# Query parts written before the key spreads, late units of a recurrence over four PSUM banks, and fills placed behind each product at a change of stage

## The chip, the cores and the metric

One core of one Trainium2 chip runs the whole program. The metric is the device time of one execution in microseconds (us); the profile is one execution taken by the hardware profiler. Engines: PE (TensorE), DVE (VectorE), ACT (ScalarE), POOL (GpSimd), SP (SyncE, which issues nearly all the DMAs); the five run their own instruction streams and meet at semaphores.

## What is computed

Four layers in a row on x of shape (4, 256, 256), each with the same context; `attend` is softmax attention with a maximum taken per row.

```python
# layer 0: 16 heads of 16, keys and values from the normalised context
Q, K, V = x @ Wq.T, ln(ctx) @ Wk.T, ln(ctx) @ Wv.T
x = x + tanh(gate) * attend(Q, K, V) @ Wo.T
# layer 1: a linear recurrence over the 256 positions, 32 heads of 8x8 state
def step(s, inp):
    a = k_l[..., :, None] * v_l[..., None, :]
    out = einsum('bhs,bhst->bht', r_l, faaaa * a + s)
    return a + w_l[..., None] * s, out
y = groupnorm(scan(step)) * gn_w + gn_b
x = x + (y * g) @ Wo.T
xc = ln(x); xk2, xr2 = mix(xc)          # with the row before
x = x + sigmoid(xr2 @ fWr.T) * (square(relu(xk2 @ fWk.T)) @ fWv.T)
# layer 2: 32 query heads of 8 on 8 key heads, additive mask, then a layer norm
# layer 3: two attentions, 16 heads of 128, 256 keys and one bias key, then an MLP
```

## The kernel before, in words

Each engine's program is written out by hand, so the order of the code is the order on the engine. The stages are: layer 0 for all four batches (`stacked_first`, 0 to 150 us), four rounds of the recurrence, one for each batch (`rwkv_block`, `main(b, ...)`, 150 to 397), layer 2 (`stacked_attention`, 397 to 675), the two wide attentions (`wide_stream`, to 1193) and the MLP. The rounds for b = 0, 1, 2 end in `meet`: each engine reports and SP (`lead`) releases them together. After b = 3 there is no meeting; its tail and the first slots of layer 2 are interleaved by hand. I call that stretch the run-out.

In layers 0 and 2 queries and keys are split into three bf16 parts, which SP writes to DRAM (`keep_keys0`, `keep_queries0`) and reads back with one feature and part to a partition row (`spread_keys0`, `spread_queries0`, `spread_rows`). A *fill* multiplies these rows for one head into bank S0 or S1; DVE then takes its row maxima (`take_maxima`, two operations, each with a short accumulator read). A fill waits until the maxima of the fill two before it are taken. Layer 2 is cut into slots; slot n from 0 on computes the transposed scores of step n, and every slot from -13 to 50 holds two fills. After the 16th fill POOL splits the maxima, PE flips them (slot -3), and ACT sends them by a DMA of its own into the query rows; slot 0 waits for it (`max_landed`).

PE also computes the keys and values of layer 3 ahead, in *units* of one 128x512 output each (`project_ahead`, lines L1109 and L1112): ACT copies a unit out of its bank (`copy_ahead`) into one of two rooms (four after the last scan), and SP stores it (`store_ahead`). A copy waits until the store that last used its room has landed. In each round of the recurrence the units after the scan are the *late* ones (`ahead_late(n)` on PE, `late(n)` on ACT): n = 0 to 4 in rounds 0 to 2, 0 to 8 in round 3. From slot -2 on layer 2 has one unit a slot, 64 in all.

The tail of round 3 is: add the output (`add_out`), normalise (`normalise_xc`), flip (`flip_xc`), mix (`fetch_xc` on ACT, `mix_channels` on DVE), the products fk, fr and fv (`project_fk`, `project_fr`, `project_fv`), and `finish_tail` on POOL. Beside it `second_batch` prepares keys and queries of layer 2's batch 1.

Of the kernel before, what the change touches and what calls it, by code (L numbers as in the profile page):

```python
# [15 lines left out]
B, S, C = 4, 256, 256  # L16
# [8 lines left out]
CHUNKS2, LEAD2 = 8, 13  # L25
# [37 lines left out]
def build(nc, d, out):  # L63
    with ExitStack() as ctx:
# [518 lines left out]
        def stacked0_sp(sp, load_first, load_rest, load_values):  # L583

            load_first()
            keep_keys0(sp, 0)
            sp.wait_ge(ones0_ready, 1)
            spread_keys0(sp, 0)
            keep_queries0(sp, 0)
            sp.wait_ge(zeros0_ready, len(q_rows0))  # L590
# [492 lines left out]
        IN_SCAN = DIM1 - 1  # L1083
# [188 lines left out]
        RING2 = [T0, T1, O0]  # L1272
        FIRST_UNIT = -2
        IN_TAIL = -9
        slots2 = {}
# [58 lines left out]
        def stacked_attention():  # L1334
            chunk_order = [(kt, j, gp) for kt in range(TQ) for j in range(2) for gp in range(2)]

            def pe_slots(pe):
# [183 lines left out]
                def second_batch():  # L1521
                    flip_x2(1)
                    keys_of(1)
                    queries_of(1)

                return slot, finish, second_batch

            def pe_program(pe):
                slot, finish, _ = pe_slots(pe)
                for at in range(IN_TAIL, LAST):  # L1530
                    slot(at)
                finish()
                meet(pe, "pe")

            def act_slots(act):
# [59 lines left out]
                def second_batch():  # L1595
                    fetch_x2(1)
                    keys2_act(act, J0, 1, 2)
                    queries2_act(act, J0, 1, 2)

# [182 lines left out]
        def rwkv_block():  # L1782
# [77 lines left out]

            def late_bank(n):
                return (S0, S1)[n % 2] if n < 4 else (J1, O1)[n % 2]
# [10 lines left out]
            def pe_program(pe):  # L1873
# [32 lines left out]
                def main(b, b_before, following, b_next):  # L1906
                    u0 = UNIT0[b]

                    def ahead_late(n):
                        u = u0 + 1 + IN_SCAN + n  # L1910
                        if n >= 2:
                            pe.wait_ge(ahead_copied, u - 1)
                        project_ahead(pe, late_bank(n), u)

# [124 lines left out]
                    if following == 2:  # L2039
                        pe.wait_ge(loaded["w2"], 16 * 5)  # L2040
                        slot, _, second_batch = slots2["pe"](pe)
                        keys2_pe(pe, J1, 0)
                        pe.wait_ge(ahead_copied, u0 + 1 + IN_SCAN)
                        queries2_pe(pe, J0)
                        for n in range(1, 4):
                            ahead_late(n)
                        pe.wait_ge(yg_ready, 1)
                        flip_out()
                        pe.wait_ge(keys2_ready, 1)
                        ahead_late(4)  # L2050
                        project_out(2)
                        second_batch()
                        flip_xc(2)
                        pe.wait_ge(ahead_copied, LATE0 + 4)
                        slot(-13)
                        slot(-12)
                        project_fk(2)
                        project_fr(2)
                        ahead_late(5)
                        slot(-11)  # L2060
                        project_fv(2)
                        ahead_late(6)
                        slot(-10)
                        for n in range(7, LATE):
                            ahead_late(n)
                    else:
                        for n in range(1, EACH[b] - 1 - IN_SCAN):
                            ahead_late(n)
# [3 lines left out]
            def act_program(act):  # L2072
# [33 lines left out]
                def main(b, b_before, following, b_next):  # L2106
                    u0 = UNIT0[b]

                    def late(n):
                        copy_ahead(act, late_bank(n), u0 + 1 + IN_SCAN + n)  # L2110

# [71 lines left out]
                    if following == 2:  # L2183
                        slot, _, second_batch = slots2["act"](act)
                        keys2_act(act, J1, 0, 1)
                        act.wait_ge(bq_ready, 1)
                        queries2_act(act, J0, 0, 1)
                    act.wait_ge(gvar_ready, 1)
                    act.activation(root, var, ACT.Sqrt).then_inc(groot_ready, 1)
                    late(1)  # L2190
                    if following == 2:
                        late(2)
                        late(3)
                        fetch_out(2)
                        late(4)
                        second_batch()
                        fetch_xc(b, 2)
                        slot(-13)
                        slot(-12)
                        square_relu(2)  # L2200
                        sigmoid_r(2)
                        late(5)
                        slot(-11)
                        fetch_fv(2)
                        late(6)
                        slot(-10)
                        for n in range(7, LATE):
                            late(n)
                    else:
# [5 lines left out]
            def pool_program(pool):  # L2215
# [28 lines left out]
                def main(b, b_before, following, b_next):  # L2244
# [31 lines left out]
                    if following == 2:  # L2276
                        split_keys2(pool, 1)
                        split_queries2(pool, 1)
                        root_of_tail(2)
                        clear_values2(pool)  # L2280
                        split_keys2(pool, 2)
# [5 lines left out]
            def dve_program(dve):  # L2287
                dve.wait_ge(loaded["ctxT"], 16)

                def main(b, b_before, following, b_next):  # L2290
# [132 lines left out]
                    if following == 2:  # L2423
                        slot, _ = slots2["dve"](dve)
                        add_out(b, 2)
                        normalise_xc(b, 2)
                        slot(-13)
                        mix_channels(2)
                        slot(-12)
                        slot(-11)  # L2430
                        slot(-10)

# [599 lines left out]
```

## Time and profile before

| what | value |
|---|---|
| median of 3 runs | 1255.22 us (1253.77 to 1258.47) |
| the profiled execution | 1257.14 us, of which its span 1255.3 |
| PE busy | 1188.2 us, 95% of the span |
| DVE, ACT, POOL busy | 793.9, 536.3, 215.9 us |
| share of PE in the chain that ended last | 84% |

The span runs from the first to the last profiled instruction; 1.84 us of the execution lie around it. A busy PE isn't a PE at its peak: PE's granted clock has two levels here, 2.4 GHz (shown as 1.00) and 1.2 GHz (0.50), and a matmul takes about twice as long at the lower one.

### The profile page before, as it was taken

How to read it: one execution, taken by the hardware profiler on the slowest of the kernel's cores; microseconds unless marked ns; L12 is line 12 of the kernel's file. 1: busy time of each engine (PE TensorE's matmuls, PEld its weight loads, DVE VectorE, ACT ScalarE, POOL GpSimd, SP SyncE). 2: the span in 40 equal slices, each digit the busy share in tenths (PEclk: the TensorE clock that was granted, in tenths of full speed). 3: DMA queues.
4: the chain of work that ended last, by engine and by line, in shares of the span. 5: the costliest groups of instructions: out<-in, count | busy, mean ns of one | idle time of the engine just before them, and what ended most of it. 6: DMA issues, size and time to landing. Idle time of an engine off the chain costs nothing.

```text
span 1255.3 us, 17672 instructions
## 1 busy us (share of the span) xinstructions
PE 1188.2 (95%) x5928; PEld 836.3 (67%) x5936; DVE 793.9 (63%) x2357; ACT 536.3 (43%) x1233; POOL 215.9 (17%) x430
## 2 busy tenths in 40 slices
PE   5989899999897899999997999999999999999998
PEld 3566554656464444444435888888888888888787
DVE  4646376868585577778755666666656666666520
ACT  3355533435354255455553434343434344343332
POOL 3240152424245101020111000000000000000000
PEclk9999999999999799999999999999999999999999
DMA  7769032021116465254249230302112121400000
GB/s 230 178 167 269 18 117 84 34 76 41 69 43 195 140 198 155 85 166 141 77 151 311 101 127 8 113 23 99 37 60 75 46 90 31 171 1 2 1 9 26
DMA packets 95033, 124.42 MB, mean 99 GB/s; under 512 B 7264, under 2 KB 72960, under 8 KB 92704
## 3 DMA queue, kind: packets, MB, share of 16 engines
q1 hardware_dynamic: 94320, 123.00, 30.7%
q8 instruction: 48, 0.79, 0.3%
q10 hardware_dynamic: 624, 0.30, 0.1%
q14 instruction: 41, 0.34, 0.1%
HBM read 79.33 MB, written 43.65 MB: 98 GB/s over the span
## 4 chain that ended last, share of the span: by engine, by line
PE 84%; DVE 4%; ACT 3%; DMA 3%; issue 2%; POOL 2%; SPq 1%; ACTq 1%; POOLq 0%; DVEq 0%
PE J L2524 9%; PE J L2544 9%; PE TT L2532 9%; PE OO L1109 5%; PE OO L1112 5%; PE TT L2508 4%; PE S L2498 4%; PE OO L2498 4%; PE J L1112 3%; PE J L323 2%; PE J L1376 2%; PE OO L2765 2%; PE S L1348 2%; PE TT L323 2%; PE J L1109 2%
## 5 line engine op out<-in xcount | busy, mean ns | idle before, releaser
L2602 ACT ACTIVATE PT<-TT 128x512 f32<-128x512 f32 x128 | 76.4, 597 | 280.2 <-PE TT L2508 280.2
L2637 POOL COPY On<-probs 128x8 f32<-128x8 f32 x128 | 29.0, 227 | 470.2 <-DVE probs L2672 440.9
L2683 DVE TENSOR_SCALAR QK<-J,cols 128x256 f32<-128x256 f32 x126 | 61.0, 484 | 68.6 <-PE J L2524 68.6
L2672 DVE TENSOR_SCALAR probs<-probs,inv 128x257 f32<-128x257 f32 x256 | 79.0, 351 | 4.5
L2508 PE MATMUL TT<-ident,probs 128*128 128x128 f32 x512 | 76.9, 273 | 2.6 <-DVE probs L2672 2.6
L1112 PE MATMUL OO<-ctxT,weights_a 128*128 128x512 f32 x144 | 70.2, 610 | 5.8 <-SPq L307 3.4
L2508 PEld LDWEIGHTS TT<-ident,probs 128*128 128x128 f32 x512 | 63.8, 141 | 16.4 <-DVE probs L2672 3.8
L2678 DVE COPY km<-TT 128x256 f32<-128x256 f32 x128 | 54.2, 423 | 30.8 <-PE TT L2532 30.5
L2386 DVE TENSOR_TENSOR_SCAN early<-km,early 128x256 f32<-128x256 f32 x64 | 64.3, 1044 | 10.9 <-ACT early L2151 10.1
L1109 PE MATMUL OO<-weights_a,ctxT 128*128 128x512 f32 x136 | 67.8, 621 | 3.4 <-SPq L307 2.9
L2544 PE MATMUL J<-early,km 128*128 128x256 f32 x256 | 65.8, 379 | 0.3 <-DVE km L2678 0.3
L2532 PE MATMUL TT<-PT,early 128*128 128x256 f32 x256 | 65.9, 380 | 0.0
L2532 PE MATMUL TT<-PT,weights_a 128*128 128x256 f32 x256 | 65.8, 379 | 0.0
L2544 PE MATMUL J<-weights_a,km 128*128 128x256 f32 x256 | 65.7, 379 | 0.0
L2664 DVE TENSOR_REDUCE maxes<-OO 128x1 f32<-128x257 f32 x128 | 48.5, 420 | 26.0 <-PE OO L2498 25.1
L2664 DVE TENSOR_REDUCE maxes<-S 128x1 f32<-128x257 f32 x128 | 48.4, 420 | 24.6 <-PE S L2498 24.6
L2594 ACT ACTIVATE probs<-S,maxes 128x257 f32<-128x257 f32 x128 | 59.3, 473 | 4.1 <-DVE maxes L2664 4.1
L2594 ACT ACTIVATE probs<-OO,maxes 128x257 f32<-128x257 f32 x128 | 59.2, 472 | 0.5 <-DVE maxes L2664 0.4
L1670 DVE CUSTOM_DVE_ANT_0 mask_b<-S,early 128x256 f32<-128x256 f32 x128 | 48.7, 417 | 15.9 <-PE S L1348 15.8
L2544 PEld LDWEIGHTS J<-weights_a,km 128*128 128x128 f32 x256 | 48.5, 190 | 7.0 <-DVE km L2678 0.3
L2532 PEld LDWEIGHTS TT<-PT,early 128*128 128x128 f32 x256 | 48.5, 190 | 7.0 <-ACT PT L2602 0.4
L2532 PEld LDWEIGHTS TT<-PT,weights_a 128*128 128x128 f32 x256 | 48.6, 190 | 6.8 <-ACT PT L2602 0.2
(423 smaller groups left out, 2623.6 us busy)
## 6 DMA issues: line engine op xcount, KB each, us to landing
wide_keys<-weights_a SPq DMA_DIRECT2D x43, 256.0 KB, 2.1
wide_values<-weights_a SPq DMA_DIRECT2D x40, 256.0 KB, 2.0
weights_a<-wide_keys SPq DMA_DIRECT2D x16, 512.0 KB, 7.1
weights_a<-wide_values SPq DMA_DIRECT2D x16, 512.0 KB, 8.6
early<-wide_keys SPq DMA_DIRECT2D x16, 512.0 KB, 8.3
early<-wide_values SPq DMA_DIRECT2D x16, 512.0 KB, 8.8
query_parts<-weights_a SPq DMA_DIRECT2D x32, 192.0 KB, 2.9
weights_a<-in_L_xattn_wv SPq DMA_DIRECT2D x2, 2048.0 KB, 9.6
```

The source lines that it names most:

```text
L1109: mm = pe.matmul(bank_[:, :], ctxT[:, k, b * S + t * P:b * S + (t + 1) * P], values_, start=(k == 0), stop=(k == KC - 1))
L1112: mm = pe.matmul(bank_[:, :], ahead_k[a][:, k, h * P:(h + 1) * P], ctxT[:, k, pair * 512:pair * 512 + 512], start=(k == 0), stop=(k == KC ...
L2386: ins = dve.tensor_tensor_scan(state[j % 2][:, half, 1:S + 1], wT[:, half, :], kv[j % 2][:, half, :], start[:, half, j:j + 1], ALU.mult, A ...
L2498: mm = pe.matmul(L_[n % 2][qt][:, 0:T], QK[:, n % 2, 0, qt * P:(qt + 1) * P], kept[g % 2][0][:, h, :], start=True, stop=True)
L2508: mm = pe.transpose(T0[:, st * S + qt * P:st * S + (qt + 1) * P], P_[n % 2][:, qt, st * P:(st + 1) * P], ident[:, :])
L2524: mm = pe.matmul(J0[:, 0:S], wide[a][0][:, k, h * P:(h + 1) * P], hidden[g % 2][:, k, :], start=(k == 0), stop=(k == KC - 1))
L2532: mm = pe.matmul(T1[:, 0:S], kept[g % 2][1][:, st, h * P:(h + 1) * P], PT[:, n % 2, st * S:(st + 1) * S], start=(st == 0), stop=(st == TQ ...
L2544: pe.matmul(J1[:, qt * S:(qt + 1) * S], avT[:, n % 2, qt * P:(qt + 1) * P], wide[a][1][:, h, :], start=(h == 0 and qt == 0), stop=False)
L2594: ins = act.activation(P_[n % 2][:, qt, 0:T], L_[n % 2][qt][:, 0:T], ACT.Exp, bias=maxes[:, qt, n % 32:n % 32 + 1], accum_out=sums[:, qt, ...
L2602: act.activation(PT[:, n % 2, :], T0[:, :], ACT.Copy).then_inc(pt3_ready, 1)
L2664: ins = dve.tensor_reduce(maxes[:, qt, n % 32:n % 32 + 1], L_[n % 2][qt][:, 0:T], AX_X, ALU.max, negate=True)
L2672: ins = dve.tensor_scalar(P_[n % 2][:, qt, :], P_[n % 2][:, qt, :], inv[:, qt, n % 32:n % 32 + 1], None, ALU.mult)
```

## The change

Three edits. First, SP writes the query parts of batch 0 before it spreads the keys. Second, in rounds 0 to 2 the late units n = 0 to 4 go to the banks S0, S1, J0, J1, S0 (before: S0, S1, S0, S1, J1), and ACT copies late unit 1 before it waits for the variance of the group norm, no longer behind the square root. Third, in the run-out: seven slots (-13 to -7) stand within round 3, before four (-13 to -10), each behind a product or a late unit; `flip_xc` stands ahead of the queries of batch 1, on ACT the mix's input ahead of those queries; DVE mixes before its first maxima; POOL clears the value pads before the root and not behind it; layer 2's first unit is in slot -1, so that its last is in slot 62 (before: -2 and 61).

```diff
             keep_keys0(sp, 0)
+            keep_queries0(sp, 0)
             sp.wait_ge(ones0_ready, 1)
             spread_keys0(sp, 0)
-            keep_queries0(sp, 0)
...
-        FIRST_UNIT = -2
-        IN_TAIL = -9
+        FIRST_UNIT = -1
+        IN_TAIL = -6
...
-            def late_bank(n):
+            def late_bank(b, n):
+                if b < B - 1:
+                    return (S0, S1, J0, J1)[n % 4]
                 return (S0, S1)[n % 2] if n < 4 else (J1, O1)[n % 2]
...
-                        if n >= 2:
+                        if b < B - 1 and n in (2, 3):
+                            pe.wait_ge(ahead_copied, u0 + 1 + IN_SCAN)
+                            pe.wait_ge(kv_ready, DIM1)
+                        elif b < B - 1 and n >= 4:
+                            pe.wait_ge(ahead_copied, u - 3)
+                        elif n >= 2:
                             pe.wait_ge(ahead_copied, u - 1)
...
                         second_batch()
                         flip_xc(2)
+                        second_queries(1)
                         pe.wait_ge(ahead_copied, LATE0 + 4)
                         slot(-13)
+                        ahead_late(5)
+                        project_fk(2)
                         slot(-12)
-                        project_fk(2)
                         project_fr(2)
-                        ahead_late(5)
                         slot(-11)
+                        slot(-10)
                         project_fv(2)
+                        slot(-9)
                         ahead_late(6)
-                        slot(-10)
-                        for n in range(7, LATE):
-                            ahead_late(n)
+                        slot(-8)
+                        ahead_late(7)
+                        slot(-7)
+                        ahead_late(8)
...
+                    if following != 2:
+                        late(1)
                     act.wait_ge(gvar_ready, 1)
                     act.activation(root, var, ACT.Sqrt).then_inc(groot_ready, 1)
-                    late(1)
...
                         fetch_xc(b, 2)
+                        queries2_act(act, J0, 1, 2)
...
+                        pool.wait_ge(yg_ready, 1)
+                        clear_values2(pool)
                         root_of_tail(2)
-                        clear_values2(pool)
...
                         normalise_xc(b, 2)
-                        slot(-13)
                         mix_channels(2)
-                        slot(-12)
-                        slot(-11)
-                        slot(-10)
+                        for at in range(-LEAD2, IN_TAIL):
+                            slot(at)
```

SP at the start of layer 0, before: the key parts are written (L533), spread (L558, L560), then the query parts written (L539) and spread (L568, L571).

```order
L533 DMA key_parts<-weights_a 128x3x256 x2
L558 DMA weights_a<-key_parts 48x1x2048 x2
L558 DMA weights_a<-key_parts 32x1x2048
L560 DMA weights_a<-key_parts 16x2048
L539 DMA query_parts<-weights_a 128x3x256 x2
L568 DMA km<-query_parts 48x1x2048 x2
```

The same place of the change:

```order
L533 DMA key_parts<-weights_a 128x3x256 x2
L539 DMA query_parts<-weights_a 128x3x256 x2
L558 DMA weights_a<-key_parts 48x1x2048 x2
L558 DMA weights_a<-key_parts 32x1x2048
L560 DMA weights_a<-key_parts 16x2048
L568 DMA km<-query_parts 48x1x2048 x2
```

The two writes of query parts moved ahead of four spreads of keys. ACT at the end of round 0, before: the last scan's copies, late unit 0, the square root (with its table load), late units 1 to 4.

```order
L410 ACTIVATE hT<-S,cols 128x256 x2
L1123 ACTIVATE weights_a<-S 128x512
L2189 ACT_TABLE_LOAD
L2189 ACTIVATE QK<-QK 128x64
L1123 ACTIVATE weights_a<-S 128x512 x3
L1123 ACTIVATE weights_a<-J 128x512
```

The same place of the change:

```order
L410 ACTIVATE hT<-S,cols 128x256 x2
L1123 ACTIVATE weights_a<-S 128x512 x2
L2200 ACT_TABLE_LOAD
L2200 ACTIVATE QK<-QK 128x64
L1123 ACTIVATE weights_a<-J 128x512 x2
L1123 ACTIVATE weights_a<-S 128x512
```

Late unit 1 moved ahead of the square root, and units 2 and 3 to J banks. PE in the run-out, before, from the flip of the normalised rows on: L1348 is a fill (four matmuls for two fills), L323 and L332 the products fk, fr, values and fv, L1112 a unit, L1384 the flip of the maxima.

```order
L315 MATMUL TT<-ident,weights_a 128x128 x4
L1348 MATMUL S<-early,weights_a 128x256 x8
L323 MATMUL TT<-weights_a,early 128x256 x4
L332 MATMUL OO<-early,weights_a 128x256 x4
L1112 MATMUL OO<-ctxT,weights_a 128x512 x2
L1348 MATMUL S<-early,weights_a 128x256 x4
L332 MATMUL J<-early,ctxT 128x64 x4
L332 MATMUL TT<-early,weights_a 128x256 x4
L1112 MATMUL J<-ctxT,weights_a 128x512 x2
L1348 MATMUL S<-early,weights_a 128x256 x4
L1112 MATMUL OO<-ctxT,weights_a 128x512 x2
L1112 MATMUL J<-ctxT,weights_a 128x512 x2
```

The same place of the change, from the product fk on:

```order
L323 MATMUL TT<-weights_a,early 128x256 x4
L1348 MATMUL S<-early,weights_a 128x256 x4
L332 MATMUL OO<-early,weights_a 128x256 x4
L1348 MATMUL S<-early,weights_a 128x256 x4
L332 MATMUL J<-early,ctxT 128x64 x4
L1348 MATMUL S<-early,weights_a 128x256 x4
L332 MATMUL TT<-early,weights_a 128x256 x4
L1348 MATMUL S<-early,weights_a 128x256 x4
L1112 MATMUL J<-ctxT,weights_a 128x512 x2
L1348 MATMUL S<-early,weights_a 128x256 x4
L1112 MATMUL OO<-ctxT,weights_a 128x512 x2
```

Two fills now stand behind each product and unit. Behind the last late unit there stood 28 fill matmuls (14 fills) ahead of the flip of the maxima, now 16 (8 fills).

## Rows read from the trace of the kernel before

**Rows 1.** Stretches: busy us of each engine, granted PE clock, DMA share, GB/s.

```profile
404.00:412.00 8.00, 4.89 (x13) 3.73 (x14) 5.09 (x15) 1.28 (x4) 3.02 (x3) 0.57 0.96 291
412.00:424.00 12.00, 12.00 (x51) 7.38 (x49) 3.33 (x20) 5.28 (x8) 2.54 (x2) 1.00 0.17 57
424.00:434.00 10.00, 6.87 (x31) 1.98 (x28) 9.84 (x55) 0.72 (x2) 1.56 (x7) 0.75 0.69 254
```

**Rows 2.** The chain of waits at the start: start us, us, what.

```profile
16.25 4.20 DMA key_parts<-weights_a
23.59 2.96 DMA query_parts<-weights_a
28.47 3.59 DMA km<-query_parts
32.72 2.89 PE OO L1109 x4
```

**Rows 3.** Timeline of DVE and SP at the start (idle before, releaser in brackets).

```profile
16.91 0.69 DVE L581 TENSOR_TENSOR weights_a<-weights_a 128x512 bf16<-128x512 f32 x1
26.61 1.82 SPq L568 DMA_DIRECT2D km<-query_parts  x3
32.54 0.42 DVE L989 CUSTOM_DVE_ANT_0 mask_b<-S,weights_a 128x256 f32<-128x256 f32 x1 [0.15 <-PE S L643]
36.07 0.42 DVE L989 CUSTOM_DVE_ANT_0 mask_b<-S,weights_a 128x256 f32<-128x256 f32 x1 [2.07 <-PE S L643]
```

**Rows 4.** Timeline at the end of round 1 of the recurrence.

```profile
259.75 3.60 PE L1109 MATMUL S<-weights_a,ctxT 128*128 128x512 f32 x8
260.12 1.28 ACT L2189 ACT_TABLE_LOAD   x1
263.59 0.26 ACT L2189 ACTIVATE QK<-QK 128x64 f32<-128x64 f32 x1 [2.19 <-DVE QK L2409]
264.39 1.98 PE L1112 MATMUL S<-ctxT,weights_a 128*128 128x512 f32 x4 [1.04 <-ACT weights_a L1123]
266.92 0.69 DVE L2422 TENSOR_TENSOR probs<-probs,km 128x512 f32<-128x512 f32 x1
268.12 0.69 ACT L1125 ACTIVATE weights_a<-J,cols 128x512 f32<-128x512 f32 x1 [0.99 <-PE J L1112]
269.74 1.98 PE L1112 MATMUL OO<-ctxT,weights_a 128*128 128x512 f32 x4 [1.65 <-SPq L307]
```

**Rows 5.** The chain of waits in the run-out.

```profile
407.50 3.78 PE TT L323 x8
415.15 0.44 PE S L1348 x4
416.43 1.78 PE TT L332 x8
422.08 1.72 PE J L1112 x4
434.82 3.41 PE OO L1109 x4
441.08 0.43 PE TT L1363 x2
```

**Rows 6.** One line's instructions: duration ns min/median/max, first and last start.

```profile
L2311 DVE SCALAR_TENSOR_TENSOR weights_a<-weights_a,cols x16: 471/479/1369, 227.0 to 407.8; 128x256 f32<-128x256 f32 x16
```

**Rows 7.** Timeline of the run-out, DMAs: the load of wv, ACT's DMA of the maxima.

```profile
423.83 0.37 SPq L2854 DMA_DIRECT2D weights_a<-in_L_xattn_wv  x1
434.21 0.76 ACTq L1548 DMA_DIRECT2D weights_a<-early  x1
```

**Rows 8.** The chain of waits in layer 0: ACT's DMA of the maxima.

```profile
99.21 7.74 DMA km<-weights_a
```

**Rows 9.** The page's DMA issues: KB each, us to landing.

```profile
wide_keys<-weights_a SPq DMA_DIRECT2D x43, 256.0 KB, 2.1
```

**Rows 10.** Timeline at the end of layer 2, its last unit.

```profile
658.05 1.98 PE L1112 MATMUL OO<-ctxT,weights_a 128*128 128x512 f32 x4
```

More of the change, by code:

```diff
@@ L1523, in second_batch @@
                     keys_of(1)
-                    queries_of(1)
-                return slot, finish, second_batch
+                return slot, finish, second_batch, queries_of
             def pe_program(pe):
-                slot, finish, _ = pe_slots(pe)
+                slot, finish = pe_slots(pe)[0:2]
                 for at in range(IN_TAIL, LAST):
@@ L1597, in second_batch @@
                     keys2_act(act, J0, 1, 2)
-                    queries2_act(act, J0, 1, 2)
                 return slot, finish, second_batch
@@ L1910, in ahead_late @@
                         u = u0 + 1 + IN_SCAN + n
-                        if n >= 2:
+                        if b < B - 1 and n in (2, 3):
[4 more added lines that the diff above has]
+                        elif n >= 2:
                             pe.wait_ge(ahead_copied, u - 1)
-                        project_ahead(pe, late_bank(n), u)
+                        project_ahead(pe, late_bank(b, n), u)
                     project_ahead(pe, O1, u0)
@@ L2040, in main @@
                         pe.wait_ge(loaded["w2"], 16 * 5)
-                        slot, _, second_batch = slots2["pe"](pe)
+                        slot, _, second_batch, second_queries = slots2["pe"](pe)
                         keys2_pe(pe, J1, 0)
@@ L2109, in late @@
                     def late(n):
-                        copy_ahead(act, late_bank(n), u0 + 1 + IN_SCAN + n)
+                        copy_ahead(act, late_bank(b, n), u0 + 1 + IN_SCAN + n)
                     copy_ahead(act, O1, u0)
@@ L2187, in main @@
                         queries2_act(act, J0, 0, 1)
+                    if following != 2:
+                        late(1)
                     act.wait_ge(gvar_ready, 1)
                     act.activation(root, var, ACT.Sqrt).then_inc(groot_ready, 1)
-                    late(1)
                     if following == 2:
+                        late(1)
                         late(2)
@@ L2197, in main @@
                         fetch_xc(b, 2)
+                        queries2_act(act, J0, 1, 2)
                         slot(-13)
+                        late(5)
                         slot(-12)
                         square_relu(2)
+                        slot(-11)
                         sigmoid_r(2)
-                        late(5)
-                        slot(-11)
+                        slot(-10)
                         fetch_fv(2)
+                        slot(-9)
                         late(6)
-                        slot(-10)
-                        for n in range(7, LATE):
-                            late(n)
+                        slot(-8)
+                        late(7)
+                        slot(-7)
+                        late(8)
                     else:
@@ L2426, in main @@
                         normalise_xc(b, 2)
-                        slot(-13)
                         mix_channels(2)
-                        slot(-12)
-                        slot(-11)
-                        slot(-10)
+                        for at in range(-LEAD2, IN_TAIL):
+                            slot(at)
                 runs(dve, "dve", main)
```

## Prediction

> **What bounds the kernel now.** PE is busy for 95% of the span and holds 84% of the chain of waits, so I looked for stretches in which PE isn't the engine that ends last, or runs at its lower clock. The chain in order of time gives three kinds of place, and they are those that the change edits; the windows by stage, the timeline and one line's durations give the numbers. All times are us.
>
> At the start SP waits for the key parts to land [rows 2], spreads them, and only then writes the query parts, waits for these too, and starts spreading them at 26.61 [rows 3]; PE's first fill stands at the end of that at 32.1. At the end of each of rounds 0 to 2 ACT sits at the square root until DVE's variance is there, with the copy of late unit 1 behind it, and PE waits 1.04 for that copy [rows 4]. In the run-out the reader is to see three windows in a row [rows 1]: at 404 to 412 PE has 4.89 of 8 us and a granted clock of 0.57 (it had stood idle for the mix), at 412 to 424 PE is busy throughout while DVE has only 3.33 of 12 us, and at 424 to 434 it's the other way: DVE has 9.84 of 10, all maxima, and PE falls to a clock of 0.75. Maxima that could lie under PE's products lie behind them.
>
> **The start.** The last of DVE's three operations that split the first queries ends at 16.91 + 0.69 = 17.60 [rows 3]. SP is then idle, since the keys land at 16.25 + 4.20 = 20.45 [rows 2]: the two writes (about 1 us of issuing) lie in that hole, and their landing, 2.96 behind the issue [rows 2], comes at about 21.6, while SP still spreads keys. The query spread so starts at about 23.1 and not at 26.61, 3.5 earlier, and the first rows land at 28.6 and not at 28.47 + 3.59 = 32.06 [rows 2]. Behind it, though, DVE is late next: its first maxima begin at 32.54 with only 0.15 of waiting [rows 3], because it splits the second batch's queries until 32.4. The gain shows one step later: the first two fills and the slow unit of 2.89 [rows 2] are then done before DVE begins, so DVE doesn't stand idle for the 2.07 ahead of its third fill [rows 3]. I take 2.0. Bounds: 0.3, if PE's clock falls in its new wait and the next unit takes 3.4 as in [rows 5] and not 1.72; 3.5, the whole shift. Nothing that follows hangs on a fixed time, so it's kept.
>
> **Late units.** ACT ends round 1 at 268.12 + 0.69 = 268.81, DVE at 267.61; the release comes 0.93 behind ACT [rows 4]. With four banks PE runs units 1 to 4 back to back from 259.75 at 1.8 each, to 266.9; the last copy ends at 267.8, and DVE then nearly ties. Gain 1.0 a round, 3.0 in three. Late unit 1's copy stands ahead of the square root now: it can begin at 261.55 and takes 0.6, the table load behind it 1.28, which gives 263.43, 0.16 ahead of the variance [rows 4]. The copies' rooms are free in time if a store lands in 2.1 [rows 9]: unit 4 needs unit 2's store, about 267. Bounds: 0 (stores that land late), 3.6 (DVE's end).
>
> **The run-out.** (a) The mix. In the old order ACT copies the second batch's queries ahead of the mix's input, and DVE mixes while POOL splits those queries: of L2311's 16 instructions the median takes 479 ns and the longest 1369, and that one is here [rows 6]. With flip and input ahead, I get the flip at 400.8 (DVE's centring, freed of POOL's clearing), xk2 at about 404.3; the product fk waited until 407.50 [rows 5].
> The Trainium skill (GPSIMD Engine Reference, section Specifications) says that GpSimd's SBUF interfaces are shared with VectorE, with contention for VectorE instructions with two SBUF inputs. The 1369 agrees. If POOL's split still overlapped the mix, xk2 would be some 1.5 later, which late unit 5, ahead of fk now, would hide.
> (b) PE from 403.4 on (queries done) to the last late unit, with no gap: 7 pairs of fills at 0.44, four units at 1.72, three products at about 1.75 (fk took 3.78 at the low clock, 1.78 is the row at the high one), the values 0.9 [rows 5], and half a microsecond where DVE is behind: 3.1 + 6.9 + 5.3 + 0.9 + 0.5 = 16.7, so 420.1. Each slot's maxima (four at 0.345, 1.38; 9.84 busy for 7 slots in [rows 1] is the same) lie under a product or unit. (c) Six slots are left that DVE bounds: 6 x 1.38 = 8.3, to 428.4; slot -1's last fill is in PE about 1 us earlier, so its unit begins at 427.4. PE is sparse for those 8 us, as it was from 424 on, so I expect the low clock and 3.4 for the unit [rows 5]: slot 0 begins at about 431, against 441.08 [rows 5]. Gain 10.0.
> (d) Given back: the unit that slot -2 no longer has stands in slot 62 now, behind what was the last unit [rows 10]. All of the stage's end hangs on the transposed scores behind it, so 1.9 comes back. PE may still be at the low clock in slot 0, another 0.7. Net 7.4. (e) The cover that must hold: slot 0 needs the maxima's DMA. POOL has the 16th fill at about 421.5, needs 2, PE flips in slot -3, ACT issues at about 425.5 (before: 434.21 [rows 7], with the load of wv, issued at 423.83, all but landed). The load now goes at about 420 and the rows of batch 1 right behind it, so the small DMA meets a full queue: 7.74 in [rows 8] (the second of two such rows 7.42), against 2.1 for a DMA that meets none [rows 9]. Landing is between 427.6 and 433.2; I take no more than 431, so no wait.
> The Trainium skill (DMA: Bandwidth & Descriptors, Queues, rings and completion order) says that each DMA engine goes round the queue rows with work, a packet at a time, and ACT's row is its own. By that alone the small DMA would hardly be held up and the sum stays; [rows 8] speak against it.
>
> **The sum.** 2.0 + 3.0 + 7.4 = 12.4, from 1257.1 (span 1255.3 and 1.84 around it) 1244.7. That execution is 1.9 above the median of the runs, 1255.2, from which it would be 1242.8; I forecast 1244, between the two. What this kernel can tell from no change is about 0.5%, 6.3 us.
>
> **The rivals.**
> 1. The maxima's DMA decides slot 0. For it: [rows 8]; against it: the load has run for 5 us by then. Slot 0 at 433.2 and another 1.5 at the low clock: the run-out gives 4 and all 9, so 1247.
> 2. The start gives little, since DVE's split ends when it did and PE's clock falls in its new wait: 0.3 for 2.0, so 1246.
> 3. The change doesn't do what it says: the maxima are only traded for PE time. DVE lags behind PE's products after all (two fills of a slot wait for the slot before), the run-out gains half, 10 becomes 5, net 2.4: 1249.
> 4. On the other side: PE stays at 1.2 GHz from 404 to slot 0, since the new order spreads its idle time over the whole run-out. Fills at 1.3 a pair, units at 3.4 and products at 3.78 [rows 5] make some 42 us of PE work there, slot 0 comes at about 446, and with 1.9 at the end and 5 from the other edits the kernel is 2 slower, 1257. It decides from some 17 us at the low clock on; against it, [rows 1] give 1.00 at 412 to 424, where PE is as dense as it will be.
>
> **How the numbers follow.** My forecast 0.60, rival 1 0.14, rival 2 0.10, rival 3 0.12, rival 4 0.04. The bounds of the terms give, downwards, 3.5 + 3.6 + 9.5 = 16.6, so 1238.6 from the median; upwards rival 3 and half of the start's loss, about 1250.5. Beyond 1248.9 (faster by 0.5%) lie half of rival 3, rival 4, and some of the rest: faster 0.82, same 0.14, slower 0.04.
>
> **What would show it.** In the profile of the changed kernel: SP's query spread at about 23.1 and DVE's third fill without its wait of 2.07; rounds that begin 1.0 sooner each, with PE's wait of 1.04 gone; in the run-out fk some 1.5 sooner and at 1.00, DVE busy under PE from 407 on, six slots of maxima in a row where there were nine, slot 0 some 15 us sooner in the execution's time (the two earlier gains included); and at the end a unit in slot 62. I'm wrong if PE's clock is low between 408 and 420, if slot 0 waits for ACT's DMA, or if the copies at the ends of the rounds wait for a store.

## The result and the profile after

The changed kernel took 1246.47 us (median of 5 runs, 1244.93 to 1252.71) against 1257.34 for the kernel before on the same chip (1253.77 to 1261.02): a ratio of 0.9933, 95% interval 0.9907 to 0.9959, so 8.4 us faster (5.2 to 11.7). A second measurement (whole_again, below) gave 1246.40 and 0.9919 (0.9891 to 0.9948). Its runs fall into two groups, three at 1244.9 to 1246.5 and two at 1252.5 and 1252.7, and the profiled execution (1252.52) is one of the slower, so below I compare stretches of it and not its end.

The run-out by windows, in the columns of [rows 1]:

```profile
404.00:412.00 8.00, 7.71 (x44) 5.69 (x42) 6.17 (x36) 3.69 (x5) 2.02 (x2) 1.00 0.72 214
412.00:421.60 9.60, 7.45 (x35) 3.33 (x33) 7.79 (x45) 2.06 (x3) 2.90 (x9) 1.00 0.59 194
421.60:433.00 11.40, 5.91 (x13) 1.69 (x12) 3.69 (x22) 2.26 (x3) 0.00 (x0) 0.52 0.81 246
433.00:439.00 6.00, 5.92 (x12) 2.38 (x13) 2.84 (x11) 1.65 (x2) 0.00 (x0) 0.50 0.00 1
```

The first window is what the change is for: PE 7.71 of 8 us at the full clock where it had 4.89 at 0.57, with DVE's maxima beneath. The third is new: PE is busy for half of it, DVE for a third, ACT for a fifth; only the DMA engines are (0.81). The fourth shows what that costs afterwards: PE dense, but at 1.2 GHz until 439.

The chain of waits of the same stretch (start us, us, what) names it, and answers to [rows 5]:

```profile
410.45 1.72 PE J L1112 x4
412.61 1.72 PE OO L1112 x4
414.77 1.72 PE J L1112 x4
...
421.42 0.23 PE J L1384 x2
...
422.09 10.86 DMA weights_a<-early
...
433.08 1.01 PE TT L1363 x2
434.09 0.85 PE S L1348 x4
434.94 3.41 PE OO L1109 x4
```

ACT's DMA of the maxima is on the chain for 10.86 us. In [rows 7] it was issued at 434.21 and slot 0 began at 441.08. The timeline of the DMA issues and of slot 0 in the changed kernel (idle time before and its releaser in brackets):

```profile
416.52 0.37 SPq L2868 DMA_DIRECT2D weights_a<-in_L_xattn_wv  x1
...
418.08 0.33 SPq L1241 DMA_DIRECT2D early<-key_parts  x1
418.45 0.84 SPq L1245 DMA_DIRECT2D km<-query_parts  x2
...
422.09 0.76 ACTq L1547 DMA_DIRECT2D weights_a<-early  x1
433.08 1.01 PE L1363 MATMUL TT<-weights_a,early 75*128 75x512 bf16 x2 [4.93 <-DMA weights_a<-early]
```

SP sends the load of wv and then the rows of layer 2's batch 1 (three DMAs, 1.44 MB) ahead of the 24 KB that slot 0 waits for. In the kernel before, the maxima went out at 434.21 [rows 7], 5 us ahead of those rows:

```profile
439.34 0.35 SPq L1241 DMA_DIRECT2D early<-key_parts  x1
```

The end of round 1, which answers to [rows 4]:

```profile
266.27 0.69 ACT L1125 ACTIVATE weights_a<-S,cols 128x512 f32<-128x512 f32 x1 [1.03 <-PE S L1112]
266.38 0.69 DVE L2438 TENSOR_TENSOR probs<-probs,km 128x512 f32<-128x512 f32 x1
267.88 1.98 PE L1112 MATMUL OO<-ctxT,weights_a 128*128 128x512 f32 x4 [1.65 <-SPq L307]
```

ACT's last copy and DVE's last operation now end 0.11 apart (266.96 and 267.07), and PE's wait of 1.04 for ACT is gone. The release, at 267.88, comes 0.92 behind ACT's end, as before (0.93).

The start, which answers to [rows 2, 3]:

```profile
23.99 1.81 SPq L568 DMA_DIRECT2D km<-query_parts  x3
31.36 0.60 PE L643 MATMUL S<-weights_a,km 128*128 128x256 bf16 x4
34.77 0.69 DVE L581 TENSOR_TENSOR weights_a<-weights_a 128x512 bf16<-128x512 f32 x1
40.70 0.42 DVE L989 CUSTOM_DVE_ANT_0 mask_b<-S,weights_a 128x256 f32<-128x256 f32 x1 [2.38 <-PE S L643]
```

The query spread is 2.6 sooner and the first fill only 0.75, since PE's own products for the second batch stand ahead of it without a gap from 26.11 on (granted clock 0.50 from 19.4 to 29.6). DVE's split of the second batch ends at 35.46 (before about 32.4), the maxima wait behind it, and a wait of 2.38 stands behind the fourth fill's maxima where 2.07 stood behind the second's.

### The profile page after: what moved, and what is told of

Read it like the earlier page. It is cut to its first block, busy times and chain, and to the rows that moved or that the text cites. A ratio compares the mean times of both kernels' runs of the same rounds, so it can differ in the third digit from the quotient of the medians.

```text
span 1250.7 us, 17685 instructions
## 1 busy us (share of the span) xinstructions
PE 1188.3 (95%) x5936; PEld 837.6 (67%) x5936; DVE 792.5 (63%) x2357; ACT 537.4 (43%) x1233; POOL 216.0 (17%) x430
## 4 chain that ended last, share of the span: by engine, by line
PE 86%; DVE 3%; ACT 3%; issue 2%; POOL 2%; DMA 2%; SPq 1%; ACTq 1%; POOLq 0%; DVEq 0%
PE J L2538 9%; PE TT L2546 9%; PE J L2558 9%; PE OO L1112 5%; PE OO L1109 5%; PE TT L2522 5%; PE S L2512 4%; PE OO L2512 4%; PE J L1112 3%; PE J L1376 2%; PE J L323 2%; PE J L1109 2%; PE OO L2779 2%; PE S L1348 2%; PE J L332 2%
## 5 line engine op out<-in xcount | busy, mean ns | idle before, releaser
L1112 PE MATMUL OO<-ctxT,weights_a 128*128 128x512 f32 x144 | 70.2, 610 | 5.8 <-SPq L307 3.3
L2692 DVE COPY km<-TT 128x256 f32<-128x256 f32 x128 | 54.2, 423 | 30.8 <-PE TT L2546 30.5
L2402 DVE TENSOR_TENSOR_SCAN early<-km,early 128x256 f32<-128x256 f32 x64 | 64.3, 1044 | 10.9 <-ACT early L2160 10.1
L2558 PEld LDWEIGHTS J<-early,km 128*128 128x128 f32 x256 | 48.3, 190 | 7.1 <-DVE km L2692 0.5
```

Source lines behind the costliest of these rows:

```text
L1112: mm = pe.matmul(bank_[:, :], ahead_k[a][:, k, h * P:(h + 1) * P], ctxT[:, k, pair * 512:pair * 512 + 512], start=(k == 0), stop=(k == KC ...
L2402: ins = dve.tensor_tensor_scan(state[j % 2][:, half, 1:S + 1], wT[:, half, :], kv[j % 2][:, half, :], start[:, half, j:j + 1], ALU.mult, A ...
L2558: pe.matmul(J1[:, qt * S:(qt + 1) * S], avT[:, n % 2, qt * P:(qt + 1) * P], wide[a][1][:, h, :], start=(h == 0 and qt == 0), stop=False)
```

## The experiments

Every profile gives the same four stretches, read from the timeline at the start of one instruction each: the first scan of round 0 (what the start and layer 0 made of it), from there to the first scan of round 3 (three rounds), from the product of layer 2's keys behind the last scan to slot 0 (the run-out), and from slot 0 to the first wide logits (what is given back in layer 2).

| kernel | median us | ratio (95%) | first scan | 3 rounds | run-out | slot 0 to logits |
|---|---|---|---|---|---|---|
| before | 1256.0 to 1257.4 | 1 | 173.70 | 178.45 | 58.99 | 234.03 |
| the change | 1246.47 | 0.9933 (0.9907 to 0.9959) | 174.46 | 174.43 | 54.41 | 237.55 |
| whole_again | 1246.40 | 0.9919 (0.9891 to 0.9948) | 171.38 | 174.40 | 53.85 | 236.63 |
| start_alone | 1256.19 | 0.9987 (0.9967 to 1.0007) | 169.65 | 178.44 | 58.50 | 234.04 |
| late_alone | 1252.61 | 0.9962 (0.9944 to 0.9980) | 172.49 | 174.45 | 59.13 | 234.03 |
| runout_alone | 1255.45 | 0.9976 (0.9960 to 0.9991) | 175.30 | 178.43 | 55.52 | 236.85 |
| late_banks_only | 1260.59 (one run) | none | 174.68 | 178.53 | 60.01 | 234.04 |
| rows_held | 1243.56 | 0.9900 (0.9879 to 0.9921) | 176.69 | 174.43 | 49.29 | 235.31 |
| wv_held | 1255.85 (one run) | none | 173.93 | 174.41 | 60.64 | 234.90 |
| held_unit_0 | 1244.03 | 0.9892 (0.9874 to 0.9910) | 174.67 | 174.41 | 48.71 | 238.03 |
| held_unit_late | 1242.47 | 0.9892 (0.9875 to 0.9909) | 171.06 | 174.42 | 48.61 | 234.90 |
| maxima_first | 1241.02 | 0.9880 (0.9858 to 0.9902) | 170.37 | 174.42 | 48.67 | 234.91 |
| maxima_first_old_start | 1245.21 | 0.9911 (0.9889 to 0.9933) | 172.33 | 174.45 | 49.30 | 235.46 |

The rounds repeat to 0.1 us from profile to profile, the run-out to about 1.5; the first scan wanders with one and the same start, by 3 with the old one (172.49 to 175.30) and by 7 with the first edit (169.65 to 176.69).

A fifth stretch, from the first wide logits to the end of the span, holds no edit and still differs: 580.4 in six profiles, that of the kernel before among them, 578.7 in whole_again and runout_alone, 580.1 in the change, 581.8 in late_banks_only, rows_held, held_unit_0 and maxima_first_old_start. What differs is PE's granted clock, which stands at 0.50 for some 3 us just behind the logits (as at 674.7 in the change), just behind 1193 (as in the kernel before), at both places or at neither. No run says why. Of the 6.0 us between the profiles of the change and of whole_again, 3.1 lie in the start, 0.6 in the run-out, 0.9 in layer 2 and 1.4 in this stretch.

### Each edit alone, and the whole again

start_alone is the first edit of the diff on the kernel before, late_alone the second, runout_alone the third; whole_again is the changed kernel unaltered.

> The kernel before with the first edit alone (query parts written ahead of the key spreads). Theory A (the prediction's): 2.0 us faster than before, and the first fill at about 30, the first maxima of DVE at about 32.5 as before, no 2.07 ahead of the third fill. Theory B, from the profile of the whole change (first fill 31.36, but DVE's split of the second batch ended at 35.46 and not 32.4, with PE at the lower clock from 20 to 29): the writes push the landing of the weights that PE's first unit waits for (20.3, before 19.5) and with it everything behind, so the start gains nothing or loses some 1 us in every execution. Theory C: the late start belongs to that one execution; then this profile shows the first unit at 19.5 and the split's end at about 32.4.

> The kernel before with the second edit alone (late units over four banks, ACT's copy of late unit 1 ahead of the square root). Prediction: 1.0 us a round, 3.0 in all; the profile of the whole change shows 1.3 a round (3.9 in all), with ACT's last copy and DVE's last multiplication ending within 0.2 of each other ahead of the release. Expected here: 3.0 to 4.0 faster, rounds 1, 2 and 3 each begin 1.3 sooner. Rival: the shorter rounds are lost again where the next round's first unit waits for its store, and the sum stays under 1.5.

> The kernel before with the third edit alone (the run-out). Prediction: net 7.4 faster. Theory after the profile of the whole change: slot 0 waits some 5 us for ACT's DMA of the maxima, and PE is at the lower clock to the end of the first unit behind it, so the edit gives about 4.5 at slot 0 and hands nearly all of it back by the end of layer 2: 0 to 3 us faster, with slot 0 at about 436 and the DMA taking 8 to 11 us. Rival: that wait belongs to the one execution that was profiled; then the DMA lands within 8 us and the edit is worth 6 to 8.

> The whole change once more, unaltered. If the five runs of the first measurement (1244.9 to 1246.5 three times, 1252.5 and 1252.7 twice) are two ways in which this program runs, this profile has an even chance to show the other one. Expected for a run near 1246: the same wait of slot 0 for the maxima's DMA (4 to 5 us) and PE at the high clock from 20 to 29 at the start, with the split of the second batch's queries ending at about 32.5. If the wait at slot 0 is gone in such a run, the wait is chance and no property of the order.

By their ratios they are 1.6, 4.8 and 3.0 us faster, together 9.4, where the whole is 8.4 and 10.2: within their intervals the edits add up. The late units give 4.0 in the rounds in every profile with the whole edit. runout_alone brings slot 0 only 3.5 sooner and gives 2.8 back, with ACT's DMA taking 9.84; whole_again, at its own median, has 9.77 there. So the wait at slot 0 belongs to the order, not to one execution. start_alone had the best start of all (PE at 1.00 from 16 to 52, first fill at 29.86 behind the rows' landing, split ended at 31.55, first scan 169.65), but its time isn't clear of no change; whole_again had the low clock only up to 24 and its split ended at 33.29. Of the theories on the start, B's late split and C's chance both hold in part: the first unit began at 20.1 to 20.6 in five of the six profiles with the edit, but at 20.22 in late_alone too, without it, and what varies most is PE's clock behind it: the split ended at 31.55 where the clock was never low, and at 34.84 to 35.46 in the three profiles where it stood at 0.50 for some 10 us up to about 29.

### What the maxima's DMA lies behind

rows_held, on the changed kernel:

```diff
                     else:
-                        sp.wait_ge(filled, SLOTS2 + 1)
+                        sp.wait_ge(max_landed, 16)
                     spread_rows(sp, b + 1)
```

> The whole change, and SP spreads the rows of layer 2's batch 1 only once the maxima's DMA has landed (before: once the 17th fill was done). Theory A: the 0.86 MB of small row pieces that SP issued some 4 us ahead of ACT's DMA are what it lies behind (9.8 to 10.9 us to land in three profiles). Then it lands 2 to 4 us behind its issue, slot 0 begins some 4 us sooner than in the whole change (run-out from the keys' product to slot 0 about 50 us, before 59.0, whole change 54), and the kernel gains another 3.5 to 5: 1242, ratio about 0.988. Theory B: it lies behind the 2 MB load of wv, which is still running then: it lands 6 us or more behind its issue and the time stays at 1246. Theory C: slot 0 would find its next wait (rows of batch 1 late for the fills of slot 3): the wait moves there and the time stays at 1246 although slot 0 is sooner.

wv_held, on the changed kernel, moves the other transfer behind the maxima:

```diff
-                                sp.wait_ge(ahead_done, UNITS)
-                                load_ahead("v")
+                                sp.wait_ge(filled, SLOTS2 + 1)
+                                spread_rows(sp, 1)
...
                     else:
-                        sp.wait_ge(filled, SLOTS2 + 1)
-                    spread_rows(sp, b + 1)
+                        sp.wait_ge(ahead_done, UNITS)
+                        sp.wait_ge(max_landed, 16)
+                        load_ahead("v")
+                    if b > 0:
+                        spread_rows(sp, b + 1)
```

> The whole change, with the other of the two large transfers taken out of the way: SP spreads the rows of batch 1 at the place of the load of wv, and loads wv only once the maxima have landed. Its unit in slot -1 then waits for wv, so slot 0 is late whatever happens (434 or later) and the time, some 1250, says nothing; what counts is how long ACT's DMA of the maxima takes. Theory A (rows): 6 to 10 us, as with both in the way. Theory B (wv): about 2 us.

The chain of waits of wv_held, with the rows alone in the way:

```profile
421.52 6.05 DMA weights_a<-early
427.64 7.55 DMA weights_a<-in_L_xattn_wv
```

The timeline of rows_held, with wv alone in the way:

```profile
418.75 0.37 SPq L2868 DMA_DIRECT2D weights_a<-in_L_xattn_wv  x1
...
424.83 0.76 ACTq L1547 DMA_DIRECT2D weights_a<-early  x1
...
426.78 3.62 PE L1109 MATMUL OO<-weights_a,ctxT 128*128 128x512 f32 x4
...
427.80 0.33 SPq L1241 DMA_DIRECT2D early<-key_parts  x1
...
430.19 1.06 PE L1363 MATMUL TT<-weights_a,early 75*128 75x512 bf16 x2
```

SP's first row DMA goes out the moment that the maxima have landed, 427.80 - 424.83 = 2.97 behind ACT's issue. So: 3.0 behind wv alone, 6.05 behind the rows alone (they are 1.44 MB, not the 0.86 of the expectation), 9.8 to 10.9 behind both; one store of 256 KB was under way in each. Theory A holds. The packets say more: in rows_held all 51 start 1.4 to 2.0 behind the issue, as they do in the kernel before (1.3 to 1.9), where wv had landed already. Here wv lands 1.5 behind the issue, so it was nearly done and cost the maxima next to nothing; a wv that is only just under way was not tried. In wv_held the 51 start 4.5 to 5.1 behind the issue. Slot 0 now begins straight behind the unit of slot -1, the run-out is 49.3 instead of 54, and theory C falls: nothing takes the wait's place, slot 0 to the logits even takes 1.3 to 2.2 less than in the whole change. By its ratio the kernel is 4.1 faster than the change by its first measurement and 2.4 by its second; the intervals overlap. Run-out and layer 2 together are 5.9 to 7.4 shorter (284.6 against 290.5 and 292.0), but behind the logits this profile is 1.7 to 3.1 longer than theirs.

### The first unit in slot 0

held_unit_0 is rows_held with `FIRST_UNIT = 0`, and the copy and store of the unit in slot 63 added behind the last slot.

> As the kernel with the held rows, and the first unit of layer 2 stands in slot 0 instead of slot -1, the last in slot 63. Slot 0 then begins when the maxima have landed and DVE is through, about 425 (3 sooner than with the held rows), but the unit at the lower clock comes just behind it, and at the end one more unit of 1.9 stands behind the last transposed scores, with its copy and store ahead of the loads of the next stage. If the tail has 1 us of idle PE to hide it, the whole is 0 to 1.5 faster than the held rows alone; if the next stage's first loads wait for its store, 1 to 2 slower.

The run-out ends 0.6 sooner than with the held rows and layer 2 takes 2.7 longer, so 2.1 are lost over both; the times (1244.03 and 1243.56, overlapping intervals) can't tell them apart. Of the 2.7, 1.45 lie between slot 0 and slot 2 (7.39 for 5.94), with the unit at the low clock (3.22), and 1.3 behind slot 2: the unit that is added at the end, some 1.9 long, is hidden for about a third.

### The start

held_unit_late is rows_held with `first_unit(0)` moved behind `queries(1, T1)` on PE, and its copy behind `fetch_queries(1, T1)` on ACT. maxima_first is rows_held with one move on DVE; maxima_first_old_start is that without the first edit of the change.

```diff
                 dve.wait_ge(mask_ready, 4)
-                split_queries(1)
                 for at in range(-LEAD0, LAST0):
...
                         take_maxima(*fill_of(at))
+                    if at == 1 - LEAD0:
+                        split_queries(1)
```

> As the kernel with the held rows, and at the start PE takes the first unit of the layer 3 values behind the second batch's keys and queries, no longer ahead of the flip of their input (ACT's copy of it likewise). Theory A (start held by the second batch's chain: unit, flip, keys, queries, ACT, DVE's split, and only then the first maxima): the split ends at about 30.5 (33.2 in the better profile of the whole change), the first maxima begin there, and the kernel gains another 2 us over the held rows. Theory B (start held by the landing of the query rows, first fill 30.4): the first maxima begin at 31 at the earliest and the gain is under 0.7.

> As the kernel with the held rows, and DVE takes the maxima of the first two fills ahead of its split of the second batch's queries. Theory A (behind the earlier fills it is this split that holds the start, and the more so the lower PE's clock is in the second batch's products): the first maxima begin at 31 whatever the clock does (32.9 to 35.4 in the profiles with the first edit), DVE doesn't stand idle for 2.4 behind its second fill, the flip of the first maxima comes at 43 to 44 (42.9 to 46.5 in those profiles), and the kernel is 1.5 to 3 faster than with the held rows. Theory B (PE's units and clock set the start): first maxima earlier, but the flip of the maxima no sooner than 45, and no gain.

> The same without the first edit: SP writes the query parts behind the key spreads, as before. The first fill comes at 32 to 33 and not at 30.5, and DVE's first maxima with it. If the first edit was worth little only because the split stood ahead of the maxima, it now costs 1.5 to 2.5 to be without it; if the query rows never held the start, this is as fast as the kernel above.

held_unit_late missed: the split ended at 32.96 and not at 30.5. PE's two products took 5.74 from 23.21 on (3.71 in start_alone), at a granted clock of 0.50 up to 27.3, and the first of DVE's three operations took 1.62 and not 0.69. With 1242.47 against 1243.56 it decides nothing. maxima_first came out as theory A has it in the maxima and the flip, and 2.5 faster than rows_held by the ratios, with intervals that overlap. "Whatever the clock does" isn't tested: in its one profile the clock was low only from 19.9 to 23.3, as in whole_again (to 23.9), and the first scan is 1.0 ahead of that one's. Its timeline on DVE:

```profile
30.16 0.42 DVE L989 CUSTOM_DVE_ANT_0 mask_b<-S,weights_a 128x256 f32<-128x256 f32 x1 [8.12 <-PE S L643]
...
31.55 0.69 DVE L577 TENSOR_TENSOR weights_a<-weights_a 128x512 f32<-128x512 f32 x1
...
32.27 0.43 DVE L579 CAST weights_a<-weights_a 128x512 bf16<-128x512 f32 x1
...
32.73 0.69 DVE L581 TENSOR_TENSOR weights_a<-weights_a 128x512 bf16<-128x512 f32 x1
...
33.33 0.42 DVE L989 CUSTOM_DVE_ANT_0 mask_b<-S,weights_a 128x256 f32<-128x256 f32 x1
```

DVE works without a gap through its first eight fills, and the third fill's maxima begin at 33.33 where they began at 36.07 [rows 3] and, in the change, at 36.75. The flip of the first maxima comes at 40.55 (before 44.38). With the old order on SP the first fill is at 32.02 instead of 29.61, and the kernel takes 1245.21 instead of 1241.02, 3.9 by the ratios (their intervals just overlap), of which the first scan shows 2.0. Of the rest the two profiles show 1.2 in the run-out and layer 2 and 1.4 behind the logits, where the two programs are the same. So once the split is out of its way the first edit is worth 2.0 at the start, and why the times differ by more stays open; before, nothing that is clear of zero. maxima_first has the lowest time: 15 us below the kernel before on that chip, 1.2%.

### The copy ahead of the square root

late_banks_only is late_alone with ACT's old order, `late(1)` behind the square root.

> The kernel before with the banks and waits of the second edit but ACT's old order (late unit 1 copied behind the square root). One look at the rounds: from the first scan of a round to that of the next it takes 56.46, 60.70 and 61.29 before, and 55.15, 59.40 and 59.88 with the second edit. If the banks alone make the gain, these come out at 55.2, 59.4 and 59.9; if the copy of unit 1 behind the root holds units 4 and the store of unit 2, each round keeps 0.5 to 1.0 of the old time.

The three rounds took 55.45, 61.40 and 61.68, together 178.53 where the kernel before has 178.45 and the whole edit 174.4. Neither expectation fits: the banks alone give 1.0 in one round and lose 0.7 and 0.4 in the others. Its timeline at the end of round 1:

```profile
263.57 0.26 ACT L2196 ACTIVATE QK<-QK 128x64 f32<-128x64 f32 x1 [2.19 <-DVE QK L2416]
...
266.43 0.69 ACT L1125 ACTIVATE weights_a<-J,cols 128x512 f32<-128x512 f32 x1 [1.63 <-DMA wide_values<-weights_a]
267.10 0.69 ACT L1125 ACTIVATE weights_a<-S,cols 128x512 f32<-128x512 f32 x1
...
268.71 3.67 PE L1112 MATMUL OO<-ctxT,weights_a 128*128 128x512 f32 x4 [1.96 <-SPq L307]
```

PE runs ahead over four banks, but ACT has two rooms: two copies in a row behind the root send two stores in a row, and the third copy waits 1.63 for the first of these to land. The copy ahead of the root spreads them. That wait is not what ate the gain, though. The last line is the release: it comes 38.58 behind the round's first scan, where it came 39.58 behind it before and 38.27 in the change. By the releases of the three rounds the banks alone bring 1.00, 1.00 and 0.80, the whole edit 1.31, 1.31 and 1.40. The gain is lost behind the release: the next round's first unit takes 3.67 and not 1.98 [rows 4], at a granted clock of 0.50 up to 272.2, and that start of a round is 1.7 longer; behind the next release it is 1.2 longer, and behind the first, with the clock at 1.00, as long as before. PE had stood idle for 1.96 and 2.30 ahead of the two releases with a low clock, for 1.82 ahead of the other, and for 1.5 to 1.7 in the kernels that keep their clock there. This is one execution, so it stays open whether the low clock comes with this order.

## Why the prediction was right, and where it wasn't

The time (1246.47, forecast 1244, range 1238.6 to 1250.5) and its sign were right, and by the ratio it is faster by over 0.5% (0.67%, interval 0.41 to 0.93%). The story behind the forecast was not: what happened at slot 0 is rival 1, to which I gave 0.14 and for which I had worked out 1247, and two terms were off in opposite directions.

**The start: 2.0 forecast, about 0.6 by the profiles.** The mean first scan is 174.0 over four profiles with the old start (before, late_alone, runout_alone, late_banks_only) and 173.5 over six with the first edit and nothing else at the start; start_alone by its ratio gives 1.6; neither is clear of zero. SP did as written, 0.9 later than forecast (23.99 for 23.1). DVE's third fill lost its wait of 2.07, but the fifth has one of 1.05 to 2.43. The step that failed is the one on DVE, "it splits the second batch's queries until 32.4": I took that end as fixed. It is the end of a chain (the first unit, the flip, two products, ACT, the split) that PE's clock stretches; it ended between 31.55 and 35.46. The term came out near its lower bound and the price of rival 2, whose split that "ends when it did" was still too kind in five of the six profiles; maxima_first shows a cure.

**Late units: 3.0 forecast, 4.0 measured** (1.31, 1.30 and 1.41 a round), above my bound of 3.6. The mechanism was right and the size too small: ACT's last copy ends 1.3 sooner in round 1 and not 1.0, and the release comes 0.92 behind it, my 0.93. DVE's end, which I took as the bound, is last by 0.11 now, and the release keeps its distance to ACT's. By late_banks_only the banks bring my 1.0 (1.00, 1.00 and 0.80 at the releases); the 0.3 to 0.6 a round that I left out come with the copy ahead of the root, which I had only cleared of harm.

**The run-out: net 7.4 forecast, 0.7 to 2.5 measured** (run-out and slot 0 to logits together: 293.02 before; 291.96, 290.48 and 292.37 with the edit). Its steps, in the change's own time, which is 3.3 ahead at that point: (a) held: the mix is free of POOL (the line's longest instruction is now 485 ns, below, where [rows 6] have 1369), fk starts at 402.05 at the full clock. (b) held: PE works with 0.3 of waiting to 416.5, forecast 420.1 less 3.3. (c) held: six slots to 425.3, forecast 428.4 less 3.3; the unit begins at 424.36 and takes 3.78, forecast 427.4 less 3.3 and 3.4.

```profile
L2327 DVE SCALAR_TENSOR_TENSOR weights_a<-weights_a,cols x16: 475/479/485, 226.5 to 401.3; 128x256 f32<-128x256 f32 x16
```

(e) failed. ACT issued at 422.09, forecast 425.5 less 3.3; but I let it land "no more than 431", with 7.74 [rows 8] as the longest, and it took 10.86. I had named what lay ahead of it, "the rows of batch 1 right behind" the load, and gave no reason for the 431; rival 1 speaks of the load alone ("the load has run for 5 us by then"). With next to nothing ahead it takes 3.0 (rows_held), where I had 2.1 [rows 9]. 4.93 of waiting, and PE's low clock up to 439, are the gain that is missing: with the rows held back slot 0 comes 9.7 to 10.4 sooner, my 10.0, and the net is 8.3 to 9.5 (the 9.5 that the range's lower end takes for the run-out has no working in the prediction).
(d) was too dear: I took back 1.9 for the unit and 0.7 for the clock, and with the rows held and the first unit in slot -1 it is 0.9 to 1.4 (rows_held, held_unit_late, maxima_first and maxima_first_old_start). In the change as made it is 2.6 to 3.5, because the unit and the first scores behind slot 0 run at 1.2 GHz.
The Trainium skill (DMA: Bandwidth & Descriptors, Queues, rings and completion order) has each DMA engine go round its queue rows a packet at a time, with several descriptors to a packet. I read that as hardly any delay for the small DMA, and the trace doesn't agree with this reading: it landed in 3.0 to 10.9, by what SP had queued. How long one turn takes no run here shows.

**The other rivals.** Rival 3 (the maxima only traded for PE time) fell: in the dense part DVE waits 0.7 a slot for PE, and isn't behind. Rival 4 (PE slow from 404 on) fell: 1.00 to 421.6. It was right in kind, though: the clock fell at 422.1 and stayed low through the DMA's wait, up to 439.

By terms the profiles give 0.6 + 4.0 + 1.4 = 6.0, the edits timed one by one 9.4, the whole 8.4 and 10.2. What separates these is within what the start (3 to 7 us from profile to profile) and the stretch behind the logits (3) can do; my sum has no term for the latter, and it stays open how much of the former is the first edit's. My 12.4 is 4 too high by the first ratio, and the step that explains most is one DMA, for which the run-out lacks some 6; holding the rows back gave the stretches these 6, but the times only 2.4 to 4.1.

## What to carry to other kernels

When a change brings a small transfer forward, list by time what is queued on every DMA queue ahead of it, and price it behind all of that; a wait on the small one's landing ahead of the large issue costs nothing if the large one has time. A wait that moves with a chain has no fixed time: before giving it a number, follow back which engine's clock it hangs on. When more banks let one engine run ahead, look at the next buffer down the line, here ACT's two rooms. And before saying which half of an edit lost a gain, cut the time at the point where the edit ends: the banks' 1.0 was there at the release of the round, and was lost behind it, at a low clock.

## What the runs showed of the hardware

The maxima's DMA has a queue of its own, and still its packets didn't move. Two windows of the DMA view of the changed kernel, each from its list of queues (q1 is SP's queue, q10 ACT's; packets, MB, share of 16 engines), from 421 to 427 and from 427 to 433:

```profile
q1 hardware_dynamic: 535, 1.89, 91.7%
q10 hardware_dynamic: 1, 0.00, 0.1%
...
q1 hardware_dynamic: 266, 1.10, 67.6%
q10 hardware_dynamic: 50, 0.02, 2.0%
```

One of its 51 packets had gone 4.9 us behind the issue, and the rest crept through beside SP's rows. With wv held back they start 4.5 to 5.1 us behind the issue, with next to nothing ahead 1.3 to 2.0.

DVE's split at the start also shows POOL's share. The cast of line L579 in the changed kernel (ns min/median/max):

```profile
L579 DVE CAST weights_a<-weights_a x3: 426/427/1261, 14.6 to 33.5; 128x512 bf16<-128x512 f32 x3
```

The long one is 1.26 to 1.27 in ten profiles, that of the kernel before among them, and in each POOL's subtraction L581 runs over its start; in held_unit_late, maxima_first and maxima_first_old_start the two don't meet, and it takes 0.43. In held_unit_late POOL's subtraction meets the split's first operation instead, a subtraction with two inputs, which takes 1.62 and not 0.69. The Trainium skill (GPSIMD Engine Reference, section Specifications) names VectorE instructions in a two-port mode, or with two SBUF inputs, as those that contend with GpSimd; the cast has one input, so by that page it would be of the first kind. That it waits the trace shows; its mode no run here does.
